# Second rope attention in three score steps with v in blocks of four head pairs, and the norms between two attentions moved into the first

## What is computed

```python
# a2: 8 heads of 128, rope, causal softmax attention, plus residual
q, k, v = x @ w_aq[h], x @ w_ak[h], x @ w_av[h]
s = x + sum_h(softmax(causal(rope(q) @ rope(k).T)) @ v @ w_ao[h])
# between: layer norm, then RMS norm with gamma
y  = (s - mean(s)) / sqrt(var(s) + 1e-5)
xn = y / sqrt(mean(y * y) + 1e-5) * gamma1
# h2: 16 heads of 64 = 8 pairs of 128 columns, rope, causal, with biases
q, k, v = xn @ q_w + q_b, xn @ k_w + k_b, xn @ v_w + v_b
attn_out = softmax(causal(rope(q) @ rope(k).T) / 8) @ v @ o_w + o_b + xn
```

## Time and profile before

| what | value |
|---|---|
| three timed runs | 1771.27, 1772.24, 1776.80 us; median 1772.24 |
| the profiled execution | 1770.54 us, its span 1768.4 us |
| busy over the span | PE 91%, PEld (weight loads) 61%, DVE 59%, ACT 57%, POOL 42% |
| a2, first projection to last value product | about 567 to 848 us |
| between, to the first scores of h2 | 848 to 885 us |
| h2, first scores to the next block | 885 to 1278 us |

### The profile page before, as it was taken

The page is one execution under the profiler, slowest core; times in us unless marked ns, Lnnn a source line. Parts: engine busy times, 40 slices in busy tenths (PEclk is TensorE's granted clock), DMA queues, the critical chain, the costliest instruction groups (busy, mean ns, idle before and its releaser), DMA issues. The chain is left out here.

```text
span 1768.4 us, 28482 instructions
## 1 busy us (share of the span) xinstructions
PE 1613.3 (91%) x9207; PEld 1084.4 (61%) x9225; DVE 1049.9 (59%) x2605; ACT 1012.7 (57%) x2188; POOL 746.8 (42%) x683
## 2 busy tenths in 40 slices
PE   5888998888798899999799999999999999888998
PEld 3556754346596677777555555555458886344786
DVE  5865775623122666666366666666558886662675
ACT  4534563553243555555466666666548887754786
POOL 1234533105252566655265555555234443021463
PEclk8999998998899999999999999999989999989999
DMA  1008323000214223232211111111046562000420
GB/s 43 2 15 179 69 73 142 1 1 30 68 34 138 60 65 68 61 69 51 78 44 47 47 40 47 47 39 49 19 144 218 219 221 87 1 1 22 148 108 25
DMA packets 61868, 124.71 MB, mean 71 GB/s; under 512 B 14258, under 2 KB 29477, under 8 KB 55228
## 3 DMA queue, kind: packets, MB, share of 16 engines
q1 hardware_dynamic: 59580, 119.24, 23.1%
q0 software_dynamic: 2144, 3.70, 0.7%
HBM read 79.05 MB, written 11.02 MB: 51 GB/s over the span
## 5 line engine op out<-in xcount | busy, mean ns | idle before, releaser
L1992 ACT ACTIVATE h_probs<-psum,h_nmax 128x512 f32<-128x512 f32 (+3 forms) x256 | 133.2, 526 | 119.0 <-DVE h_nmax L2073 64.1
L2073 DVE CUSTOM_DVE_ANT_0 psum<-psum,h_mask 128x512 f32<-128x512 f32 (+3 forms) x256 | 122.6, 511 | 83.3 <-PE psum L1876 80.4
L917 ACT ACTIVATE psum<-psum,f_b 128x512 f32<-128x512 f32 x200 | 132.3, 662 | 30.0 <-PE psum L874 30.0
L1804 POOL TENSOR_TENSOR h_swapped<-h_swapped,rope_tables 128x512 f32<-128x512 f32 x64 | 81.8, 1278 | 153.6 <-DMA h_swapped<-h_raw 153.6
L840 POOL TENSOR_TENSOR e_lo<-e_gated,e_hi 128x512 fp32r<-128x512 f32 x59 | 76.0, 1289 | 150.3 <-ACT e_hi L929 150.3
L2425 ACT ACTIVATE a_probs<-psum,a_nmax 128x512 f32<-128x512 f32 (+3 forms) x128 | 67.5, 527 | 120.7 <-DVE a_nmax L2500 70.3
L2246 POOL TENSOR_TENSOR a_swapped<-a_swapped,a2f_a_tables 128x512 f32<-128x512 f32 x64 | 82.0, 1281 | 127.1 <-DMA a_swapped<-a_raw 127.0
L952 DVE TENSOR_TENSOR e_lo<-psum,e_hi 128x512 fp32r<-128x512 f32 x168 | 114.8, 683 | 24.9 <-ACT psum L917 24.9
L126 PE MATMUL psum<-rope_tables,mean_w 128*128 128x256 f32 x482 | 118.3, 396 | 7.0 <-ACT h_raw L1982 2.8
L1883 PEld LDWEIGHTS psum<-ident,h_probs 128*128 128x128 f32 x640 | 71.4, 141 | 80.4 <-issue 52.8
L1883 PE MATMUL psum<-ident,h_probs 128*128 128x128 f32 x640 | 115.1, 287 | 1.7 <-ACT h_probs L1992 1.4
(11 more groups left out here) (501 smaller groups left out, 4135.7 us busy)
## 6 DMA issues: line engine op xcount, KB each, us to landing
e_gate<-gates SPq DMA_DIRECT2D x39, 1024.0 KB, 4.7
a_swapped<-a_raw SPq DMA_DIRECT2D x128, 128.0 KB, 2.3
h_swapped<-h_raw SPq DMA_DIRECT2D x256, 64.0 KB, 2.0
e_gate<-gates SPq DMA_DIRECT2D x16, 512.0 KB, 8.0
f_w<-in_l_experts SPq DMA_DIRECT2D x32, 128.0 KB, 4.6
slots<-a_empty SPq DMA_DIRECT2D x1, 2600.0 KB
f_w<-in_l_experts SPq DMA_DIRECT2D x9, 256.0 KB, 4.9
e_got<-slots SPq DMA_DIRECT2D x7, 325.0 KB, 4.2
```

The source lines that it names most:

```text
L917: nc.scalar.activation(to, hidden_bank(n), ex.act_func, **bias(n)).then_inc(act_ready, 1)
L1992: nc.scalar.activation(probs[:, j % 4, 0:(q + 1) * P], ring[j % RING][:, 0:(q + 1) * P], ACT.Exp, scale=-1.0, bias=nmax[:, j % 8:j % 8 + 1 ...
L2073: nc.vector.tensor_tensor_reduce(s, s, mask[:, (QT - 1 - q) * P:], scale=-1.0, scalar=-SENT, op0=ALU.add, op1=ALU.min, accum_out=nmax[:, j ...
```

## The change

`rope_attention` is renamed `pair_attention` and keeps only the branches for two heads per unit (`heads = 2`). A unit has three steps in place of four: query tile 3; tiles 2 and 0 side by side in one bank; tile 1. v is made in 32 blocks, each for one tile of 128 tokens and four head pairs, with split operands:

```diff
+    STEPS = 3
+    parts = (((3, 0),), ((2, 0), (0, 3)), ((1, 0),))
...
+        vs = st.sb("v", [P, QT, G, P])
+        wv_hi, wv_lo = (st.sb(f"wv_{n}", [P, G, P], F32R) for n in ("hi", "lo"))
...
+                def value_block(m):
...
+                    if to is not acc:
+                        pe.wait_ge(raw_ready[0], min(max(m, AHEAD + 1), NU))
+                    nc.tensor.matmul(to, x_hi[:, at], wv_hi[:, of, :].rearrange("p g d -> p (g d)"), start=True, stop=False)
+                    nc.tensor.matmul(to, x_hi[:, at], wv_lo[:, of, :].rearrange("p g d -> p (g d)"), start=False, stop=False)
+                    nc.tensor.matmul(to, x_lo[:, at], wv_hi[:, of, :].rearrange("p g d -> p (g d)"), start=False, stop=True).then_inc(v_psum, 1)
...
+                    for q, at in parts[s]:
+                        for h in range(heads):
...
+                            if q == parts[s][-1][0]:
+                                mm.then_inc(s_ready, 1)
```

PE's work between the transposes (two slots a step, six a unit in place of eight); the value products are one group:

```diff
-                def values(U, key_tiles):
...
+                def values(U):
+                    if U + 3 <= NU:
+                        pe.wait_ge(raw_ready[1], min(U + 4, NU))
...
+                    for k in range(QT):
...
                 def spread_sums(U):
 
                     pe.wait_ge(wide_ready, U + 1)
-                    if not merged and U + 3 < NU:
-                        pe.wait_ge(v_ready, U + 4)
-                    elif merged and U + 3 < NU:
+                    if U + 3 < NU:
                         pe.wait_ge(raw_ready[0], U + 4)
...
+                    if slot == 0:
+                        if U == 0:
+                            value_block(0)
+                        if V < NU:
+                            project_q(V)
                     if slot == 1 and V < NU:
                         project_k(V)
...
+                    if U == 0 and slot in (2, 3, 4):
+                        value_block(slot - 1)
...
                     if U >= 1:
+                        if slot == 2:
+                            spread_sums(U - 1)
                         if slot == 3:
-                            values(U - 1, (0,))
-                        if slot == 4:
-                            spread_sums(U - 1)
-                            values(U - 1, (1,))
+                            values(U - 1)
+                        if slot == 4 and block_of(U) < blocks:
+                            value_block(block_of(U))
                         if slot == 5:
-                            values(U - 1, (2, 3))
-                        if slot == 7:
                             out(U - 1)
...
-                keep_busy(core, pe, 6, 10 if merged else 4)
+                keep_busy(core, pe, 6, 8)
```

```diff
+                    U = V - AHEAD
+                    if U - 3 >= G:
+                        pe.wait_ge(norm.scaled_out, (U - 3) // G)
+                    if U - 2 >= G:
+                        pe.wait_ge(norm.plain_out, (U - 2) // G)
...
-                        if U > 1 and U % G == 1:
-                            turn_back(U // G - 1)
+                        for k in range(2):
+                            if U > G and U % G == 2 + k:
+                                pe.wait_ge(raw_ready[1], U + AHEAD)
+                                norm.turn(pe, U // G - 1, k, misc[1])
...
-                keep_busy(core, pe, 0, 8)
-                turn_back(B - 1)
+                keep_busy(core, pe, 0, 20)
+                for k in range(2):
+                    norm.turn(pe, B - 1, k, misc[k])
...
+                    if n == 2 and U > G and U % G == 1:
+                        norm.invert(act, U // G - 1)
+                    if n == 3 and U > G and U % G == 3:
+                        norm.copy_scaled(act, U // G - 1, misc[1])
...
+                    if U > G and U % G == 1 and n == 0:
+                        dve.wait_ge(added, G * (U // G))
+                        norm.moments(dve, U // G - 1, total[:, U // G - 1, :, :])
+                    if U > G and U % G == 1 and n == 3:
+                        norm.scale(dve, U // G - 1, 0, total[:, U // G - 1, :, :])
+                    if U > G and U % G == 2 and n == 0:
+                        norm.scale(dve, U // G - 1, 1, total[:, U // G - 1, :, :])
+                    if U > G and U % G == 2 and n == 3:
+                        norm.copy_plain(dve, U // G - 1, misc[1])
```

The first two waits are in `project_k(V)`, in place of the one on `sum_done`. For the last sequence all these steps follow at the end of a2. SP issues the loads of h2's weights and biases (ten DMAs) inside a2, after the swaps of unit 8. The second block has no norms of its own:

```diff
-            after_a2 = layer_norm(core, sh, "n2a", xc=(5, 3, 4, 7), var=(0, 1))
-            g1 = Norm(core, sh, "g1", core.x, xn, center=False, eps_col=0, gamma=core.gammas[:, 0, 0:1], src_ready=after_a2.out_ready, var=(5, 3, 4, 7))
-            rope_attention(core, "h2", rope, Head(core, after_a2, g1, rope), x=xn, heads=2)
+            attn2(core, xn, rope)
+            recycle(core)
+            pair_attention(core, "h2", rope, Ready(Ahead()), x=xn)
```

More of the change, by code:

```diff
@@ L1764, in rope_attention, with block_bank @@
         acc = core.psum[:, 7, :]
-        def step_items(K):
-            return [(K * heads + h, h) for h in range(heads)]
+        def block_bank(m):
+            return acc if m in (0, 2) else misc[0]
         with nc.Block() as block:
@@ new lines, in scores @@
+                    for q, at in parts[s]:
+                        for h in range(heads):
+                            rows = slice(h * dv, (h + 1) * dv)
+                            mm = nc.tensor.matmul(ring[(K * heads + h) % RING][:, at * P:(at + q + 1) * P], qs[rows, U % 3, q * P:(q + 1) * P],
+                                                  ks[rows, U % 3, 0:(q + 1) * P], start=True, stop=True)
+                            if q == parts[s][-1][0]:
+                                mm.then_inc(s_ready, 1)
@@ L2076, in copy_t @@
[L2076 to L2084 removed]
+                        dve.wait_ge(qk_ready, 2 * V - 1)
@@ L2175, in token_attention, with __init__, wait, sync @@
+class Ready:
+    def __init__(self, ahead):
+        self.ahead = ahead
+    def wait(self, engine, b):
+        pass
+    def sync(self, sp):
+        self.ahead.sync(sp)
+    def gpsimd(self, pool):
+        pass
+    def tensor(self, pe):
+        pass
+    def scalar(self, act):
+        self.ahead.scalar(act)
+    def vector(self, dve):
+        pass
+def token_attention(core, name, front, head, *, x, gamma, scaled, following):
     nc = core.nc
@@ L2579, in _ @@
                         normalise(U - 1)
-                    if n == 3 and U > 1 and U % G == 1:
-                        sum_out(U // G - 1)
+                    if U > G and U % G == 1 and n == 0:
[7 more added lines that the diff above has]
+                        norm.copy_plain(dve, U // G - 1, misc[1])
                 inverse_sums(NU - 1)
                 normalise(NU - 1)
-                sum_out(B - 1)
+                dve.wait_ge(added, NU)
+                norm.moments(dve, B - 1, total[:, B - 1, :, :])
+                for k in range(2):
+                    norm.scale(dve, B - 1, k, total[:, B - 1, :, :])
+                norm.copy_plain(dve, B - 1, misc[0])
 class RopeFront(Ahead):
```

416 lines of the change are left out of this document (214 added, 202 removed).

## The result

The changed kernel takes 1782.06 us (median of 11 runs), the kernel before 1772.24 in the same series: a ratio of 1.0047 (95% interval 1.0024 to 1.0069). By the ratio it is slower by about 8 us, by the medians by 9.8, where 6 us faster was forecast. The profiled execution has a span of 1780.3 us for 1768.4.

What follows compares the result with a forecast made beforehand. PE's list was taken to bound the second attention. Second attention -13.1, between the attentions -7.0 and first attention +14.5 sum to -5.6 us: 1764.9 from the profiled 1770.5, median forecast 1766, range 1753 to 1777.

Steps and rivals of the forecast that it cites:

- DVE and ACT do no more than before: Second attention: two part maxima, exponentials and copies replace two whole ones, so these engines get no extra work.
- The lock: First attention: a DVE operation waits beside POOL; one wait of 1.0 us in each scale, costing 0.9 and 0.7.
- The steady period: Second attention: 11.7 us a unit for 12.09, including a 0.36 us wait before spread_sums for ACT's copy of q.
- stands close behind: Second attention: POOL's widening ends at 4.9 us, 0.2 before PE's new place for spread_sums; an argument against PE's sum deciding.
- Rival (b): Second attention: PE's own sum decides, period 11.25 to 11.3 us, 12 us more gain, 1754; chance 0.17.
- rival (c): Second attention: POOL's rotation becomes the bound; with a period of 12.3, 17 us more, 1783; chance 0.1.
- 4.84 a sequence: First attention: cost of the new norm's work for each of three sequences, +14.5 us in all.
- the second turn: First attention: one extra turn on PE for each of the first sequences, 0.44 us.
- Rival (a): Its own description isn't in the text given; the reflection ties it to two waits on the first scale, price 6.8; chance 0.2.
- Between the attentions: From first to second attention: filler +5.6, whole-batch norms gone -14.35, four more filler calls 1.75; sum -7.0 us.
- at full rate: Ahead of the second attention's first scores: four more filler calls take 1.75 us, 3.4 if the clock stays at 1.2 GHz.
- both signs by which the forecast was to be called wrong: Second attention's period leaving 11.5 to 11.9 us, or the first attention growing by under 10 or over 18 us.

Runs made afterwards that it cites:

- splits_early: The changed kernel with the splits of weights and sequences moved to step n == 1 from n == 2: 1770.37 us, ratio 0.9981 to the kernel before.
- all_moved: The changed kernel with splits and norm turns earlier, filler shortened and moved, spread_sums later and POOL's widening earlier: 1739.91 us, ratio 0.9823 to the kernel before.
- widen_late: all_moved with POOL's widening back behind the whole rotation, spread_sums staying at slot 3: 11.29 us a unit in one execution.
- turns_early: The changed kernel with the new norm's two turns at n == 1 and copy_scaled and copy_plain at n == 2: 1774.24 us, ratio 1.0011.
- attention_only: The kernel before with only the new second attention, old norms kept: 1766.26 us (0.9973), then 1771.9 us (0.9997) when run again.

## Why the prediction was wrong

**The step that failed** is in the second attention: "DVE and ACT do no more than before", and with it the count of units 0 to 5 at the steady period, -0.6 and 5 x -0.39. The amount of work is indeed the same: in the steady part 7.4 us a unit on either engine, for 7.7 before. But `round_w`, `low_w`, `round_x` and `low_x` had moved from n == 1 to the end of a unit of three steps, ahead of the next unit's minima, and no line of the prediction follows them there; the description of the change doesn't name the move either. That start took 85.3 us where 73.7 was forecast. Of the 11.6, 8.9 is this place (shown by `splits_early`; the two ranges above leave 6 to 12). Of the rest, 1.6 is unit 0, where the first widening still came 17.05 behind the first scores for a forecast 15.5, and 1.1 is in units 1 to 5. In unit 0 the trace of `splits_early` has the inverse sums ready at 15.6; the widening stands behind POOL's whole rotation, which began at 10.4 for 9.7 before. With the widening ahead of the rotation's last sum it came at 15.8 (`all_moved`) for 17.05 (`widen_late`), but unit 5 at 75.7 in both.

**The lock was weighed in the wrong attention.** The prediction priced it for `scale` and not for the subtractions. Here the two-operand subtraction of 512 columns took 0.69 us alone and 1.77 beside POOL, and `scale`, with one tensor operand, this, first beside POOL and then alone (timeline of the changed kernel, POOL and DVE):

```profile
667.55 1.30 POOL L2332 TENSOR_TENSOR a_swapped<-a_swapped,a2f_a_tables 128x512 f32<-128x512 f32 x1
667.91 2.89 DVE L2204 TENSOR_SCALAR a_norm_out<-sum_fm,a_norm_mean_var,a_norm_inverse 128x128 f32<-128x128 f32 x4
668.93 1.27 POOL L2337 TENSOR_TENSOR a_k<-a_rot,a_swapped 128x512 f32<-128x512 f32 x1
...
671.61 1.08 DVE L2204 TENSOR_SCALAR a_norm_out<-sum_fm,a_norm_mean_var,a_norm_inverse 128x128 f32<-128x128 f32 x4
```

The rule of the Trainium skill (SBUF — State Buffer, section "SBUF: two separate sides"), that these two engines exclude each other at their shared ports for a whole instruction, agrees with both: the subtraction ended 0.55 us behind the end of POOL's sum, and four scalings took 2.89 us for 1.08.

**The steady period was right**, 11.74 for 11.7 (11.67 to 11.80 over eleven profiles with `spread_sums` in slot 2), with the wait of 0.39 on ACT's copy of q that was named. That POOL "stands close behind" was right as well: 8 of the 28 waits, 5.3 of 13.0 us, are for its widening. Rival (b)'s number, 11.25, is what the loop gives once the two waits are away; rival (c), a loss of 17 us by the rotation, did not come: its late halves came in single units, the longest wait being 1.6 us.

**Inside the first attention**: 4.84 a sequence was forecast. Between the first and the last `normalise` the trace has 262.4 us for 247.6, +14.9, so 4.95. Its terms come out less well than their sum: `project_k` behind `copy_scaled` 1.7 for 2.0; exponentials late by 1.6 ((7.7 - 2.9) / 3) for the 2.4 of `moments` and the scales; PE's own work 1.2 longer for the 0.44 of the second turn; and 0.4 of wait for `a_raw` (L2403) that no term names. So that 4.84 fits 4.95 is in part luck. `moments` itself took 0.84 + 0.38 for 1.4. Rival (a)'s two waits on the first scale came (1.6 to 1.8 us more than alone), none fell on the second, and its price of 6.8 did not come true.

**Between the attentions**: 31.05 us for 37.1, -6.0 for -7.0. Up to the first projection it is -8.8, as forecast. What is missing is the clock behind it: the eight calls took 6.2 us, where four more "at full rate" made 5.2.

**The sum.** With these two parts at +8.8, the whole change hung on the 13.1 us of the second attention; it gave 1.4 (six profiles: -4.7 to +0.1). The chance for "slower" was 0.15, most of it on a mechanism of the steady part. No rival looked at the start, where each list differs from the steady one, and both signs by which the forecast was to be called wrong stayed in their bounds (11.74 and +14.9). From -5.6 to the profile's +11.9 it is 17.5 us: 11.6 of them are the start, 3.6 the router.

## What to carry to other kernels

When a loop gets fewer steps, write out its first units as well as a steady one: the work that exists only there (splits, loads, roundings) has to find a step with slack on its own engine, and the right step here was one where the engine waits anyway. Before `splits_early` and `turns_early` the change cost 8 us; with the same operations in other places, and the filler and the sums placed by the trace, it gains 33 in the median (`all_moved`, 1739.9 for 1773.4), 27 in the parts. And put filler into a wait, right behind the last work, not after the wait: after it the filler ran here at a granted clock of 0.58, and the scores came 4.0 us behind the k that they needed.

## What the runs showed of the hardware that was not expected

- Filler behind 6.5 us of idle PE ran at a granted clock of 0.58, so mostly at 1.2 GHz: eight calls in 6.23 us. Placed right behind the last matmuls, twenty ran in 8.79, at 1.00.
- DVE's subtraction with two SBUF operands took 1.77 us for 0.69 beside POOL: it began 0.12 behind POOL's sum at 922.44 and ended 0.55 behind the end of it. POOL's operation grew a little too, to 1.34 and 1.44 from 1.27.
- The same code ahead of the first mark took 591.9 to 612.4 us, and the router without added filler 27.5 to 32.6. A difference under some 5 us shows in a part's length in the trace sooner than in the total: `attention_only` was 0.9973 in one series and 0.9997 in the next.
